# One slot-attention and expert kernel: reordering its preparation, from the first normalised tokens to the second pair's first attention product

## What is computed

```python
h = layernorm(x)
slots = h                                   # 4 batches, 1024 slots of 256 each
Pn = rmsnorm(ctx);  k, v = Pn @ Wk.T, Pn @ Wv.T
for _ in range(3):
    q = rmsnorm(slots) @ Wq.T
    attn = softmax(q @ k.T / 16, axis=slots)        # over the 1024 slots
    attn = attn / (sum(attn, axis=context) + 1e-6)  # the column sums
    slots = gru_cell(attn @ v, slots, wih, whh, bih, bhh)
x = x + tanh(g_xattn) * slots
x = x + tanh(g_ffn) * moe(layernorm(x))     # 16 experts, 512 tokens each, and a shared expert
```

## Time and profile before

| | us |
|---|---|
| three timed runs | 1148.86, 1148.21, 1146.03 |
| their median | 1148.21 |
| the profiled execution, whole | 1144.72 |
| the span of its trace | 1143.0 |
| matrix engine busy in the span | 1094.6 (96%) |

### The profile page before, as it was taken

One profiled execution on the slowest core, in us unless ns is written; L12 is line 12 of the kernel. 1 busy time (PEld: TensorE's weight loads), 2 busy tenths in 40 slices (PEclk: granted clock), 3 DMA queues, 4 the chain that ended last, 5 costly groups with the idle time before them and its releaser, 6 DMA issues.

```text
span 1143.0 us, 17692 instructions
## 1 busy us (share of the span) xinstructions
PE 1094.6 (96%) x6087; PEld 939.8 (82%) x6087; DVE 777.4 (68%) x1501; ACT 548.9 (48%) x830; POOL 331.0 (29%) x351
## 2 busy tenths in 40 slices
PE   6689999999999998999999999999999999999996
PEld 4567788888888786888888888888888888888896
DVE  6783577777778886788656656666656666656663
ACT  3354445454545863333454545545445454445542
POOL 6103334343403400000212323323223324233332
PEclk9798999999999999999999999999999999999998
DMA  7420101010126433212294344444344453354421
GB/s 239 99 49 1 38 1 37 1 37 1 39 90 167 147 118 82 37 19 38 41 286 118 104 139 134 104 132 109 118 143 112 119 138 95 129 147 99 127 34 20
DMA packets 61195, 105.39 MB, mean 92 GB/s; under 512 B 12000, under 2 KB 50144, under 8 KB 56800
## 3 DMA queue, kind: packets, MB, share of 16 engines
q1 hardware_dynamic: 43792, 83.04, 22.7%
q0 software_dynamic: 16512, 21.50, 11.7%
q10 hardware_dynamic: 848, 0.29, 0.1%
HBM read 74.11 MB, written 21.27 MB: 83 GB/s over the span
## 4 chain that ended last, share of the span: by engine, by line
PE 86%; DVE 8%; ACT 2%; issue 1%; DMA 1%; SPq 1%; POOL 0%; DVEq 0%; ACTq 0%
PE wide L1270 29%; PE down L1284 15%; PE wide L844 14%; PE wide L1123 8%; PE down L1135 4%; PE down L899 3%; PE wide L851 2%; PE wide L853 2%; PE wide L1316 2%; PE side L1256 1%; PE side L1107 1%; PE down L1330 1%; PE side L303 1%; DMA x_raw<-in_x 1%; PE side L923 1%
## 5 line engine op out<-in xcount | busy, mean ns | idle before, releaser
L2219 DVE SCALAR_TENSOR_TENSOR hid<-wide,b_up,silu 128x512 f32<-128x512 f32 x120 | 90.1, 751 | 164.1 <-PE wide L1270 155.0
L1270 PE MATMUL wide<-xt_hi,w_hi 128*128 128x512 f32 x480 | 189.0, 394 | 0.8
L1270 PE MATMUL wide<-xt_lo,w_hi 128*128 128x512 f32 x480 | 187.7, 391 | 0.0
L1270 PE MATMUL wide<-xt_hi,w_lo 128*128 128x512 f32 x480 | 186.9, 389 | 0.0
L815 POOL DMA_INDIRECT out_tokens<-y,idx_out x64 | 104.8, 1637 | 230.7 <-DVE y L2200 183.5
L1638 ACT ACTIVATE silu<-wide,b_gate 128x512 f32<-128x512 f32 x120 | 82.1, 684 | 147.1 <-PE wide L1270 147.1
L1284 PE MATMUL down<-w_hi,hid_hi 128*128 128x256 f32 x480 | 136.5, 284 | 0.0
L1284 PE MATMUL down<-w_lo,hid_hi 128*128 128x256 f32 x480 | 135.7, 283 | 0.0
L1284 PE MATMUL down<-w_hi,hid_lo 128*128 128x256 f32 x480 | 135.7, 283 | 0.0
L1647 ACT ACTIVATE hid_hi<-hid 128x512 fp32r<-128x512 f32 x120 | 76.0, 633 | 99.8 <-DVE hid L2219 99.8
L2170 DVE TENSOR_TENSOR w_lo<-raw,w_hi 128x768 fp32r<-128x768 f32 x128 | 121.6, 950 | 2.6 <-ACT w_hi L1612 2.5
(11 more groups left out here) (318 smaller groups left out, 2277.1 us busy)
## 6 DMA issues: line engine op xcount, KB each, us to landing
raw<-in_w_expert SPq DMA_DIRECT2D x32, 1536.0 KB, 6.8
x_raw<-in_x SPq DMA_DIRECT2D x16, 256.0 KB, 7.6
out_tokens<-slots SPq DMA_DIRECT2D x16, 256.0 KB, 3.8
token_rows<-work SPq DMA_DIRECT2D x8, 512.0 KB, 3.0
out_tokens<-y POOLq DMA_DIRECT2D x8, 512.0 KB, 5.9
attn<-rms_c SPq DMA_DIRECT2D x24, 128.0 KB, 2.3
attn<-expo SPq DMA_DIRECT2D x24, 128.0 KB, 2.3
x_first<-in_x SPq DMA_DIRECT2D x8, 256.0 KB, 3.1
```

What stands on the lines that cost most here:

```text
L1270: last = nc.tensor.matmul(bank[:, f % 2, :], w[f // HALF_F][:, f % HALF_F, (c + k) * P:(c + k + 1) * P], x_[:, k, :], start=(m == 1), stop ...
L2219: nc.vector.scalar_tensor_tensor(hid[:, f % 2, :], eup[:, f % 2, :], b_up[:, bass.ds(e, 1), f:f + 1].rearrange("p a b -> p (a b)"), silu[: ...
```

## The change

Nothing is computed in another way. Instructions are moved, and some change their engine. (Lines of the kernel after are a few higher: L851 is L855, L923 is L931, L1868 is L1878.)

1. GpSimd waits for n_x, the end of VectorE's normalise(0), before it splits whh.
2. Matrix engine: the 18 slots products of unit (0,0,0,0) stand ahead of column_sums(0), turn_rec(0) and spread_rec(0), and its attention products behind them.
3. ScalarE: normalise(3) follows normalise(1) at once, and value_weights(3) comes after first_high(0) and first_high(2).
4. Second pair: VectorE normalises groups 4 and 5 ahead of the first GRU group and ScalarE groups 6 and 7 behind units 0 and 1. VectorE takes first_slots(4). The late splits, the spreading of the factors and the scaling of the scores are spread otherwise over the first units. The gathering of the second statistics (aggregate, L1843) comes ahead of csum_reciprocal(0), and one more first_stats with it.
5. Matrix engine: turn_rms(1) and spread_rms(1, h) come earlier, and scores(1) is in two halves, one before unit (0,0,1,1), one within it. exponentials(1) comes one step earlier on ScalarE, and token_sum(1) ahead of GRU group 2 on VectorE.
6. SP: in move_attention, in all iterations, the two DMAs of a half that read rms_c are started when ScalarE has written it (a_attn), and only the two that read expo wait for VectorE (v_alo).
7. The load of the two tanh gates g_in goes from ScalarE's queue to the end of SP's loads, and their tanh to a later place.

The diff, cut to its core:

```diff
-        NORM_BY_VECTOR = (0, 2, 6, 7)
-        NORM_BY_SCALAR = (1, 3, 4, 5)
+        NORM_BY_VECTOR = (0, 2, 4, 5)
+        NORM_BY_SCALAR = (1, 3, 6, 7)
...
                 def move_attention(s, pair, h):
...
+                    sp.wait_ge(a_attn, 2 * s + h + 1)
+                    for b in range(2):
+                        sp.dma_start(attn[rows_of(b), pair, b, half].bitcast(F32), rms_c[rows_of(b), h, :]).then_inc(d_attn[h], 16)
                     sp.wait_ge(v_alo, 2 * s + h + 1)
                     for b in range(2):
-                        sp.dma_start(attn[rows_of(b), pair, b, half].bitcast(F32), rms_c[rows_of(b), h, :]).then_inc(d_attn[h], 16)
                         sp.dma_start(attn[rows_of(1 - b), pair, b, half].bitcast(F32), expo[rows_of(b), half]).then_inc(d_attn[h], 16)
...
+                pool.wait_ge(n_x, 1)
                 pool.wait_ge(l_whh, 16)
                 nc.gpsimd.tensor_copy(whh_hi[:, :, :], whh_sb[:, :, :]).then_inc(p_wlo, 1)
...
                 scores(0, 0, (2, 4), True)
+                pe.sem_inc(s_ss, G)
+                pe.wait_ge(p_wlo, B + 2)
+                gru_unit(0, 0, 0, 0, None, ("slots",))
                 column_sums(0)
                 turn_rec(0)
                 spread_rec(0)
-                pe.sem_inc(s_ss, G)
-                pe.wait_ge(p_wlo, B + 2)
-                gru_unit(0, 0, 0, 0)
+                gru_unit(0, 0, 0, 0, None, ("attention",))
                 gru_unit(0, 0, 0, 1, lambda: turn_first(4))
+                turn_rms(1)
                 turn_first(5)
                 gru_unit(0, 0, 1, 0, lambda: turn_first(6))
+                spread_rms(1, 0)
                 turn_first(7)
                 pe.wait_ge(s_s0, G)
-                scores(1, 1, (G - 1, G))
-                turn_rms(1)
-                gru_unit(0, 0, 1, 1, lambda: spread_rms(1, 0))
+                scores(1, 1, (G - 1, G), halves=(0,))
                 spread_rms(1, 1)
+                gru_unit(0, 0, 1, 1, lambda: scores(1, 1, (G - 1, G), halves=(1,)))
                 sum_squares(pe, G, 0, 0, (v_ms, 2))
...
                 normalise(1)
-                value_weights(3)
+                normalise(3)
                 first_high(0)
                 first_high(2)
-                normalise(3)
+                value_weights(3)
                 copy_rms(0, 0, True)
...
-                gru_unit(0, 0, 0, 0, None, (lambda: normalise(4),), (lambda: normalise(5),))
-                gru_unit(0, 0, 0, 1, None, (lambda: first_slots(4),), (lambda: first_slots(5),))
-                gru_unit(0, 0, 1, 0, None, (lambda: first_slots(6),), (lambda: first_slots(7),))
-                gru_unit(0, 0, 1, 1, lambda: copy_rms(1, 0), (new_high,), (lambda: copy_rms(1, 1),))
-                gru_unit(0, 0, 2, 0, None, (lambda: slots_high(0, 0, 1),), (lambda: exponentials(1),))
+                gru_unit(0, 0, 0, 0, None, (), (lambda: normalise(6),))
+                gru_unit(0, 0, 0, 1, None, (lambda: first_slots(5),), (lambda: normalise(7),))
+                gru_unit(0, 0, 1, 0, lambda: first_slots(6), (),
+                         (lambda: copy_rms(1, 0), lambda: first_slots(7), lambda: copy_rms(1, 1)))
+                gru_unit(0, 0, 1, 1, None, (new_high,))
+                gru_unit(0, 0, 2, 0, lambda: exponentials(1), (lambda: slots_high(0, 0, 1),))
...
-                first_stats(range(NT + 10, NT + 15))
+                first_stats(range(NT + 11, NT + 16))
+                aggregate(stats1, mv1, var1)
                 csum_reciprocal(0)
                 spread_reciprocal(0)
-                first_stats(range(NT + 15, NT + 16))
...
-                aggregate(stats1, mv1, var1)
                 reciprocal_roots(1, mv1, var1, rstd1, rtmp1, shift1)
-                gru_group(0, 0, 0, (lambda: normalise(6), lambda: normalise(7)),
-                          (lambda: late_split(4), lambda: late_split(5)))
-                gru_group(0, 0, 1, (lambda: late_split(6), lambda: late_split(7), lambda: spread_steps(1)),
-                          (lambda: scale_scores(1, 0), lambda: scale_scores(1, 1), lambda: maximum(1)))
-                gru_group(0, 0, 2, (lambda: token_sum(1), lambda: csum_reciprocal(1)), (lambda: spread_reciprocal(1),))
-                gru_group(0, 0, 3, (lambda: attention_half(1, 0), lambda: attention_half(1, 1)),
-                          (lambda: attention_lo(1, 0), lambda: attention_lo(1, 1)))
+                normalise(4)
+                normalise(5)
+                gru_group(0, 0, 0, (lambda: first_slots(4), lambda: late_split(4)),
+                          (lambda: spread_steps(1), lambda: late_split(5)))
+                late_split(6)
+                gru_group(0, 0, 1, (lambda: late_split(7), lambda: scale_scores(1, 0)),
+                          (lambda: scale_scores(1, 1), lambda: maximum(1)))
+                token_sum(1)
+                gru_group(0, 0, 2, (lambda: csum_reciprocal(1),), (lambda: spread_reciprocal(1),))
+                gru_group(0, 0, 3, (lambda: attention_half(1, 0), lambda: attention_half(1, 1),
+                                    lambda: attention_lo(1, 0), lambda: attention_lo(1, 1)))
```

34 lines of the change are left out of this document (19 added, 15 removed).

## The result

| | us |
|---|---|
| before, median of 4 runs beside it | 1147.38 (1146.03 to 1148.86) |
| after, median of 4 runs | 1134.12 (1133.41 to 1134.35) |
| ratio | 0.9883, 95% interval 0.9866 to 0.9900 |
| profiled execution after (span) | 1134.24 (1132.5) |

The change makes the kernel 13.3 us faster, twice the 6.6 that I forecast, and the time lies 0.9 us under the range. The sign was right, the size was not. The profiled executions lie 10.5 us apart, the medians 13.3: the executions of before scatter (1143.6 to 1148.7 in 19 runs made later), and its profiled one is among the quick ones. More on this stands under the part on the prediction.

The account below looks back on a forecast made before the run. The matrix engine was taken to bound the kernel behind 135.5 us, so only what lies ahead was priced: −1.7 −0.7 +1.9 −6.1 = −6.6 us, from the median 1148.21 to 1141.6 us, range 1135 to 1146.5.

Parts of the forecast that it names:

- Stretch 1: From the start to the first column sums (49.8 us before); forecast 1.7 us shorter, to 48.1.
- Stretch 2: From the first column sums to unit 0's first attention product (62.3 us before); forecast 0.7 us shorter.
- Stretch 3: From unit 0's attention to the second column sums (107.8 us before); forecast 1.9 us longer.
- Stretch 4: From the second column sums to the second pair's first attention product (135.5 us before); forecast 6.1 us shorter.
- Bound: Behind 135.5 us the matrix engine is busy; gains or losses ahead of it go through to the end one for one.
- I leave the rest as it is: Behind 135.5 us, nothing changes of itself: no wait for attention DMAs in the trace; forecast 0.
- The hold of normalise(2): VectorE, before the first column sums: GpSimd's two instructions hold it up by 4.99 us, between bounds 0 and 4.99.
- The terms g_in and tanh cost nothing: Moving the load of two values and their tanh, to where ScalarE waits for the scores' maximum, priced at nothing.
- Group 0's split starts as before: ScalarE, first_slots(0) to last split: with normalise(3) ahead, only groups 2 and 1 follow without the gap; 2.3 us less.
- (a): Before the first column sums: normalise(2) isn't held, GpSimd waits for it; −11.7 us in all, 1136.5; chance 0.28.
- (b): Second column sums to second pair's attention: the clock's gain doesn't come; −2.1 us in all, 1146.1; chance 0.15.
- (c): Matrix engine's two new idle stretches each bring 10 us of half clock; +4.1 us in all, 1152.3; chance 0.07.

Follow-up runs that it names:

- before_gin: Kernel before with only the g_in load moved to the end of SP's loads and its tanh moved later; 1144.07 us, ratio 0.9983.
- before_pad: Kernel before with one more instruction in the matrix engine's stream ahead of its expert loop (s_ss count split in two); 1142.52 us, ratio 0.9965.
- before_slots_ahead: Kernel before with only the 18 slots products moved ahead of the first column sums; 1145.49 us, ratio 0.9994.
- before_poolwait: Kernel before with only GpSimd's wait for normalise(0) added; 1146.38 us, ratio 1.0001.
- best_four_edits: Changed kernel with GpSimd waiting for normalise(2) too, first_slots(7) earlier, aggregate behind attention_lo(0,1), and vw_own earlier; 1125.93 us, ratio 0.9825.
- best_three_edits: Changed kernel with GpSimd waiting for normalise(2) too, first_slots(7) ahead of unit 2's tanh, and aggregate behind attention_lo(0,1); 1128.94 us, ratio 0.9856.
- after_no_poolwait: Changed kernel without GpSimd's wait on n_x; 1134.24 us, ratio 0.9893.
- after_wait2: Changed kernel with GpSimd waiting for normalise(2) as well (n_x of 2); 1130.42 us, ratio 0.9848.

## Why the prediction failed where it did

The forecast missed 6.7 us of the gain. Stretch 1 gave 3.7 more than forecast, stretch 2 1.0 less, stretch 3 0.8 more, stretch 4 nothing, and the experts 3.2 that the sum didn't have.

- **Bound**: right, what is gained ahead of the second pair's attention goes through. **"I leave the rest as it is"**: this step failed, by the 3.2 us of the expert loop. The table hides it. Its −0.2 from there to the end is the sum of two things that I didn't have: −3.2 from the loop, and +2.9 ahead of the loop, where the trace has two short falls of the clock. These are, in the kernel after,

```profile
364.20:372.20 8.00, 6.08 (x28) 5.11 (x28) 7.86 (x14) 5.63 (x10) 6.11 (x8) 0.79 0.63 199
420.20:436.20 16.00, 12.36 (x53) 9.22 (x52) 8.04 (x22) 6.23 (x9) 0.00 (x0) 0.89 0.45 131
```

and the same places, 239 and 295 us behind the second pair's attention, in the profiled execution of before:

```profile
374.50:382.50 8.00, 6.17 (x36) 5.09 (x35) 7.83 (x16) 6.21 (x11) 7.57 (x10) 1.00 0.66 208
430.50:446.50 16.00, 12.31 (x66) 9.64 (x65) 10.88 (x31) 6.85 (x10) 0.00 (x0) 1.00 0.37 102
```

  That execution had neither. The traces of before_gin and before_pad have both, that of before_slots_ahead has one, that of before_poolwait none. The changed kernel and its ten variants have both, best_four_edits has one, best_three_edits none. Where a trace has neither and the new loop (best_three_edits), the time from the second pair's attention to the end is 1004.6; with both and the old loop (before_gin) it is 1011.2; before (old loop, no falls) and after (new loop, both) lie between, at 1007.5 and 1007.25. So the profiled execution of before lacked the falls, and its distance to the one of after hides the loop's 3.2 us. That the medians don't is argued from the runs' mean clock: of 48 runs of before, the fourteen at 0.982 took 1147.5 us on average, and the nine at 0.985 to 0.987 took 1144.8. Whether the changed kernel is ever free of the falls isn't shown.
- **Stretch 1, −1.7 forecast, −5.4 measured.** The hold of normalise(2) was the right choice between two bounds, 4.35 for 4.99. In rows, the root comes 1.7 sooner (forecast 0), first_slots(0) behind it 0.1 later (forecast +0.7), and the last split behind that 3.8 sooner (forecast −2.3). So two other steps failed. "The terms g_in and tanh cost nothing" was wrong by 1.5 to 1.7 us. And "Group 0's split starts as before": I priced part 3 as the 2.06 us of normalise(3), and overlooked that value_weights(3) stood ahead of first_high(0) with a wait of 3.35 us for the matrix engine. The term was 2.3; measured it is 3.8 against before, and 5.2 with GpSimd's wait in both. The wait was in the trace of before, ahead of the earlier trace rows's first row.
- **Stretch 2, −0.7 forecast, +0.3 measured.** All its terms (column sums −1.1, gathering +1.4, DMA starts −0.9) are of the chain of VectorE and SP. That chain did get shorter: SP's last start comes 0.7 sooner behind the column sums' start (9.4 for 10.1). But the DMA engines then set the end, and the landing takes 3.33 instead of 2.34. The DMA share of 0.96 in the earlier trace rows was the hint. That the miss is only 1.0 is luck: the sum of the terms happened to be small.
- **Stretch 3, +1.9 forecast, +1.1 measured.** The mechanism as named: to the scores 2.6 more than before (23.7 for the 24.4 forecast), from there on 1.5 less (forecast 1.4).
- **Stretch 4, −6.1 forecast and measured.** Undoing part 5's end gives 2.8 us of it back in this stretch and puts the second pair's attention 3.9 later (129.2 for 125.25); the attention's DMA wait of 1.58 stays gone. The clock's part of the forecast, 4.5, is what is left of the 6.1 without that wait.
- **Rivals.** (a) fell by the 7.02 us row, after_no_poolwait and after_wait2. Its number, 1136.5, was nearer than mine by luck, since other causes made the gain; and of the 5.1 that it subtracts only 4.7 were worked out. (b) and (c) fell: the second column sums are at clock 1.00. (c)'s premise is half true: behind the two new idle stretches the products run at half clock for 3.3 and 3.4 us, where I took 4 and (c) 10 (0.89 over 46.6 us is 10 us at half, the rest of it within the second idle).
- **The Trainium skill**, "SBUF — State Buffer", section "SBUF: two separate sides": its exclusive lock fits the 4.35 us of hold. What it leaves open, whether GpSimd gets in between VectorE instructions that wait for nothing, the trace answers: it does, within normalise(2). The page also says that a DMA isn't slowed by compute. The trace agrees: the attention's last DMA took 3.33 us behind the value weights' DMAs (share 1.03) and 2.33 when these had landed, with VectorE's steps beside it both times.

Added up in medians, single edits undone: g_in 1.6, part 3 3.7, part 5's end 3.2, GpSimd's wait 0, DMA starts 0, gathering 0, one more instruction ahead of the loop 3.2 to 3.9. That is 11.7 to 12.4 of 13.3. Each share is good to 1 or 2 us only: by the ratios, each against its own runs of before, g_in is 3.0, part 3 4.5, part 5's end 3.4 and GpSimd's wait 1.1, with intervals of 2 us to either side, and the sum is then over 13.3. The new division of the second pair's work and the halved scores weren't undone apart, and the products ahead (part 2) only in the kernel before.

## What to carry to other kernels

A wait that takes one engine off another's path pays only if it is released behind the last instruction that shares the path: here one count further was worth some 2 to 3 us, and the wait as written nothing. When a stretch of the profile has a DMA share near 1, price the bytes in flight ahead of the transfer that is waited for as a second bound beside the compute chain. And of an instruction that is moved, ask first what it waits for and who stands behind it; here its own duration was the smaller part. And a loop that nothing in the change touches can still change its time: compare it in both traces before the gain is ascribed.
